# In a first layer's last image, the norm's weights and the residual sum move from GpSimd to VectorE, and projections use two PSUM pairs

## The chip, the cores and the metric

The kernel is one program on one core of a Trainium2 chip. The core has four compute engines that run side by side, each through its own instructions in order: TensorE (PE in the rows) multiplies matrices, VectorE (DVE) and ScalarE (ACT) work elementwise and reduce, GpSimd (POOL) works elementwise on SBUF. SyncE (SP) issues the transfers (DMA). An instruction can wait for a semaphore to reach a count, and raise one when it is done. The metric is the device time of one execution in microseconds (us), the median of several.

## What is computed

Two layers on x, 16 images of 128x128 positions with 128 channels, all f32. The change lies in the first, a linear attention with a norm behind it and the input added:

```python
qkv = einsum('bxyc,cf->bxyf', groupnorm(x), w_qkv)      # 4 heads of 32
q = softmax(q, over the head) * scale;  k = softmax(k, over the positions)
context = einsum('bhdn,bhen->bhde', k, v)
out = einsum('bhde,bhdn->bhen', context, q) @ w_out + b_out
x1 = x + (out - mean) / sqrt(var + eps) * g_ln + b_ln    # mean, var over channels
```

The second layer takes x1, normed in groups, through 7x7 convolutions with gates, a scan of 8 steps and a last product. The sums for its norm come out of the first layer.

## The kernel before

The first layer (`layer0`) cuts an image into 16 chunks of 1024 positions (8 tiles of 128), 256 chunks in all. It is a pipeline over three images: while image i+2 is loaded and turned (`ga`), image i+1 gets its keys, queries and context (`gb`), and image i its output (`gc`). Each engine has its own program of 16 steps `n` an image. In step gc of the last image nothing of ga is left, and nothing of gb after its second step, so only this remains:

- TensorE: the gram of chunk gc-3 (`gram_of`, L468: x1 times itself, summed over the image in psG), behind a wait for x1 of that chunk (`s_x1`); then the projection of chunk gc-1 (`project`, L527: queries times the folded matrix M, into psO, which the rows call psProj, one pair of PSUM banks), behind a wait for `s_y`, that the chunk before has been read out of psO.
- ScalarE: the square of the projection (L615).
- VectorE: row sums of the squares of chunk gc-2 (L650), then, behind GpSimd's `rstd`, y = psO times rstd (`scale_rows`, L656), into the single buffer y, behind `s_x1` of the chunk before.
- GpSimd: rstd from the row sums in two operations (L801, L804, 128x8), then y times the norm's weights (L812), then the input chunk xc plus y (L817), which raises `s_x1`. The bias of the norm is accounted for elsewhere.
- SP: loads of xc, one chunk of the input for each step, four buffers; and, behind `s_x1`, the stores of x1 in four or seven transfers.

Two pairs of banks, psR[0] and psR[1], serve turns, keys and queries while there are images behind; in the last image they are idle from the third step on. The order in every engine is that of the code; nothing is scheduled elsewhere. After the last chunk a block of another kind starts (`corner_block`), behind the last stores.

Of the kernel before, what the change touches and what calls it, by code (L numbers as in the profile page):

```python
# [25 lines left out]
ALU = mybir.AluOpType  # L26
ACT = mybir.ActivationFunctionType
AX = mybir.AxisListType

P = 128  # L30
IMGS, HT, WD, C = 16, 128, 128, 128
# [10 lines left out]
TPC = 8  # L42
CT = TPC * P
NCH = N // CT
# [207 lines left out]
def layer0(nc, x, w_qkv, w_out0, b_out0, g_ln, head_d, x1_d, x1s_d, x1e_d, ident, group, sums2):  # L252

    CHUNKS = IMGS * NCH
# [3 lines left out]
    with ExitStack() as ctx:  # L258
# [4 lines left out]
        qT = [sb(f"qT{n}", [P, CT]) for n in range(NCH)]  # L263
        xa = [sb(f"xa{k}", [P, TPC, C]) for k in range(2)]
        xb = [sb(f"xb{k}", [P, TPC, C]) for k in range(2)]
        xc = [sb(f"xc{k}", [P, TPC, W1]) for k in range(4)]
# [3 lines left out]
        sqo = sb("sqo", [P, TPC, C])  # L270
        y = sb("y", [P, TPC, C])
# [7 lines left out]
        grow = sb("grow", [P, C])  # L279
# [13 lines left out]
        M = sb("M", [P, C])  # L293
# [16 lines left out]
        psR = [ps(f"psR{k}", [P, CT]) for k in range(2)]  # L310
        psO = ps("psProj", [P, CT])
# [8 lines left out]
        s_xc = [sem(f"b_xc{k}") for k in range(4)]  # L320
# [38 lines left out]
        s_y = sem("b_y")  # L359
        s_yg = sem("b_y_gained")  # L360
        s_x1 = sem("b_x1")
# [6 lines left out]
        def live(img, chunk):  # L368
            return not isinstance(img, int) or 0 <= chunk < CHUNKS

        def image_live(img):
            return not isinstance(img, int) or 0 <= img < IMGS

        def upto(count):
            return max(0, min(count, CHUNKS)) if isinstance(count, int) else count

# [68 lines left out]
        def _(pe):  # L445
# [74 lines left out]
            def project(img, n, gc):  # L520
                m = (n - 1) % NCH
                if m == 0:
                    pe.wait_ge(s_mready, img + 1)
                pe.wait_ge(qt_taken, gc)
                pe.wait_ge(s_y, upto(gc - 1))
                for t in range(TPC):
                    mm = nc.tensor.matmul(psO[:, t * C:(t + 1) * C], qT[m][:, t * P:(t + 1) * P], M[:],  # L527
                                          start=True, stop=True)
                mm.then_inc(o_ready, 1)

# [54 lines left out]
        @block.scalar  # L585
        def _(act):
            def image(img, steps):
                for n in range(steps):
                    ga, gb, gc = indices(img, n)
                    if live(img, gb - 2):  # L590
                        act.wait_ge(qt_ready, gb - 1)
                        act.wait_ge(o_ready, upto(gc - 1))
                        nc.scalar.copy(qT[(n - 2) % NCH][:], psR[n % 2][:]).then_inc(qt_taken, 1)
                    if live(img, gb - 1):
                        act.wait_ge(e_ready, gb)
                        act.wait_ge(ctx_done, upto(gb - 1))
                        nc.scalar.copy(ek[:].rearrange("p t c -> p (t c)"), psR[(n + 1) % 2][:]).then_inc(ek_ready, 1)
                        act.wait_ge(q_subbed, gb)
                        v = q[(n - 1) % 2]
                        nc.scalar.activation(v[:], v[:], ACT.Exp).then_inc(s_qexp, 1)  # L600
                    if live(img, gb):
                        act.wait_ge(s_nmax, gb + 1)
                        act.wait_ge(e_ready, upto(gb))
                        nc.scalar.activation(ekT[:], psR[n % 2][:], ACT.Exp, bias=nmax[:, n + 1:n + 2],  # L604
                                             accum_out=ksum_c[:, n:n + 1]).then_inc(k_exped, 1)
                        nc.scalar.activation(corr[:, n:n + 1], nmax[:, n:n + 1], ACT.Exp, bias=nmax[:, n + 1:n + 2],
                                             scale=-1.0).then_inc(s_corr, 1)
                    if n == 0 and image_live(img):
                        act.wait_ge(s_m, img * 7 + 3)
                        nc.scalar.activation(ctxg[:], psC[:, 128:256], ACT.Identity, bias=norm_old[:, 1:2],  # L610
                                             scale=norm_old[:, 0:1]).then_inc(s_m, 1)
                    if live(img, gc - 1):
                        act.wait_ge(o_ready, gc)
                        act.wait_ge(s_vsum, upto(gc - 1))
                        nc.scalar.activation(sqo[:].rearrange("p t c -> p (t c)"), psO[:], ACT.Square  # L615
                                             ).then_inc(s_sqo, 1)
                    if live(img, ga):
                        act.wait_ge(t_taken, ga)
                        act.wait_ge(t_ready, ga + 1)
                        act.wait_ge(q_ready, upto(gb + 1))  # L620
                        if image_live(img + 1):
                            act.wait_ge(s_red, img + 2)
                        src = psR[n % 2][:]
                        nc.scalar.activation(junk[:], src, ACT.Square, accum_out=part_sums[:, 1, n:n + 1])
                        nc.scalar.activation(xT[n][:], src, ACT.Identity, accum_out=part_sums[:, 0, n:n + 1]
                                             ).then_inc(t_taken, 1)

            all_images(act, image)

        @block.vector  # L630
        def _(dve):
            t = Tally(dve, s_chain)
# [19 lines left out]
            def scale_rows(n, gc):  # L652
                dve.wait_ge(s_rstd, gc - 1)
                dve.wait_ge(s_x1, upto(gc - 2))
                rs = rstd[:, n % 2, :].unsqueeze(2).to_broadcast([P, TPC, C])
                nc.vector.tensor_tensor(y[:], psO[:].rearrange("p (t c) -> p t c", c=C), rs, ALU.mult  # L656
                                        ).then_inc(s_y, 1)

            def reduce_sums(gb):
                dve.wait_ge(t_taken, gb + NCH)  # L660
# [91 lines left out]
            def image(img, steps):  # L752
                for n in range(steps):
                    ga, gb, gc = indices(img, n)
                    if live(img, gc - 2):
                        row_sums(img, n, gc)
                    if n == 0 and image_live(img):
                        nc.vector.tensor_copy(norm_old[:], norm[:])
                    if n == 0 and image_live(img + 1):
                        reduce_sums(gb)  # L760
                    if n == 1 and image_live(img):
                        dve.wait_ge(s_m, img * 7 + 5)
                        nc.vector.tensor_tensor(ctxT[:], psC[:, 256:384], head[:], ALU.mult).then_inc(s_m, 1)
                    if live(img, gc - 2):
                        scale_rows(n, gc)
                    if n == 1 and image_live(img):
                        dve.wait_ge(s_m, img * 7 + 7)
                        dve.wait_ge(o_ready, img * NCH)
                        nc.vector.tensor_tensor(M[:], psC[:, 384:512], brow[:], ALU.add).then_inc(s_mready, 1)
                    if n == 2 and image_live(img - 1):  # L770
                        take_gram(img, gc)
                    if n == 0 and image_live(img + 1):
                        norm_weights(img, gb)
                    if n == 0 and live(img, gb - 1):
                        add_up(n, gb)
                        mean_context(img, gb)
                    if n == 0 and image_live(img + 1):
                        split_bias(img)
                    if live(img, gb):
                        max_k(n, gb)  # L780
                    if live(img, gb - 1):
                        sum_q(n, gb)
                        if n:
                            add_up(n, gb)
                    if live(img, gb):
                        centre_q(n, gb)
# [4 lines left out]
        def _(pool):  # L791
# [4 lines left out]
            def image(img, steps):  # L796
                for n in range(steps):
# [8 lines left out]
                    if n == 0 and image_live(img + 1):  # L806
                        pool.wait_ge(s_st, (img + 1) * 5 + 4)
                        nc.gpsimd.tensor_tensor(norm[:, 0:1], var[:], half[:, 0:1], ALU.pow).then_inc(s_pow, 1)
                    if live(img, gc - 2):
                        m, owner = (n - 2) % NCH, img if n >= 2 else img - 1  # L810
                        pool.wait_ge(s_y, gc - 1)
                        nc.gpsimd.tensor_tensor(y[:], y[:], grow[:].unsqueeze(1).to_broadcast([P, TPC, C]), ALU.mult  # L812
                                                ).then_inc(s_yg, 1)
                        pool.wait_ge(s_yg, gc - 1)
                        pool.wait_ge(s_xc[m % 4], owner * (4 * NCH) + m // 4 * 16 + 16)
                        v = xc[m % 4][:, :, 0:C]
                        nc.gpsimd.tensor_tensor(v, v, y[:], ALU.add).then_inc(s_x1, 1)  # L817
# [735 lines left out]
```

## Time and profile before

| | us |
|---|---|
| median of 3 runs | 6883.95 |
| the three runs | 6856.88 to 6893.54 |
| the profiled execution, its time | 6909.09 |
| its span, first to last instruction | 6907.3 |
| last image's stretch, first projection to last x1 | 3522.28 to 3655.95 |

All rows are of the profiled execution, times counted from its span's start. A chunk number below is that of the whole run: the last image has chunks 240 to 255. PEclk is the granted clock of TensorE as a share of 2.4 GHz.

### The profile page before, as it was taken

What the parts mean: (1) busy time and instruction counts of PE and PEld (TensorE: products, weight loads), DVE (VectorE), ACT (ScalarE), POOL (GpSimd) and SP (SyncE); (2) the same over time, 40 slices, a digit from 0 to 9 for tenths busy, and PEclk for the clock granted to TensorE, in tenths of its full rate; (3) what the DMA queues carried; (4) which work ended last, traced back from release to release, by engine and by line L of the source; (5) the groups of instructions that cost most, each with busy time, mean ns of one, the idle gap of its engine ahead of it and who ended that gap; (6) DMA issues with size and microseconds to landing.
All of it is one profiled execution on the core that took longest, in us unless ns stands there. A gap on an engine that the chain in (4) does not pass through costs nothing. (4 is left out here: it accounts for less than half of the span.)

```text
span 6907.3 us, 144255 instructions
## 1 busy us (share of the span) xinstructions
PE 5912.3 (86%) x51796; PEld 5278.5 (76%) x51796; DVE 4477.4 (65%) x5283; ACT 3641.9 (53%) x4872; POOL 4068.1 (59%) x3608
## 2 busy tenths in 40 slices
PE   6799999999999999999871378888888888888898
PEld 5678888888888888888761277777777777777787
DVE  6367777777777777777744556666666666666652
ACT  5655556555555555555421355555555555555552
POOL 0146666666666666666671676676666666666640
PEclk8899999999999999999985699999999999999996
DMA  5356667666677666676561589999999899999985
GB/s 129 122 166 208 198 207 216 198 205 201 202 211 209 203 202 201 204 216 205 169 176 50 148 218 247 243 255 249 257 244 255 241 255 255 244 249 250 251 231 154
DMA packets 1239334, 1441.35 MB, mean 209 GB/s; under 512 B 142960, under 2 KB 1025396, under 8 KB 1238516
## 3 DMA queue, kind: packets, MB, share of 16 engines
q1 hardware_dynamic: 1238516, 1431.07, 73.4%
q8 instruction: 437, 7.16, 0.4%
q14 instruction: 381, 3.12, 0.1%
HBM read 999.09 MB, written 431.64 MB: 207 GB/s over the span
## 5 line engine op out<-in xcount | busy, mean ns | idle before, releaser
L1283 PE MATMUL psC<-wide,xhl 128*128 128x256 bf16 x6144 | 1042.9, 280 | 198.6 <-DVE xhl L1451 170.4
L1220 POOL TENSOR_TENSOR stage<-stage,nrow 128x1024 f32<-128x1024 f32 x256 | 652.3, 2549 | 597.7 <-DMA stage<-x_by_block_row 583.0
L1280 PE MATMUL psC<-wide,xhl 128*128 128x192 bf16 x6144 | 868.6, 251 | 0.0
L1237 POOL COPY down<-xhl 48x448 f32<-48x448 f32 x512 | 522.5, 1021 | 545.6 <-PE psC L1289 486.4
L812 POOL TENSOR_TENSOR y<-y,grow 128x1024 f32<-128x1024 f32 x256 | 604.0, 2359 | 323.7 <-DVE y L656 323.7
L1283 PEld LDWEIGHTS psC<-wide,xhl 128*128 128x128 bf16 x6144 | 593.6, 115 | 210.0 <-issue 195.1
L1456 DVE SCALAR_TENSOR_TENSOR xhl<-xhl,psC 128x512 f32<-128x512 f32 x512 | 348.9, 682 | 540.4 <-ACT xhl L1372 539.9
L1387 ACT ACTIVATE hT<-psH 128x512 f32<-128x512 f32 x512 | 305.2, 596 | 700.0 <-PE psH L1325 699.7
L823 POOL TENSOR_TENSOR q<-q,qinv 128x1024 f32<-128x1024 f32 x256 | 490.1, 1914 | 309.4 <-DVE qinv L730 309.4
L1372 ACT ACTIVATE xhl<-psC 128x512 f32<-128x512 f32 x512 | 304.8, 599 | 664.0 <-PE psC L1289 662.5
L1289 PE MATMUL psC<-narrow,down 128*128 128x96 bf16 x6144 | 532.5, 211 | 143.0 <-DMA narrow<-toeplitz_narrow 94.9
L1280 PEld LDWEIGHTS psC<-wide,xhl 128*128 128x128 bf16 x6144 | 641.8, 115 | 14.4
L656 DVE TENSOR_TENSOR y<-psProj,rstd 128x1024 f32<-128x1024 f32 x256 | 313.5, 1225 | 516.1 <-POOL rstd L804 516.1
L615 ACT ACTIVATE sqo<-psProj 128x1024 f32<-128x1024 f32 x256 | 263.2, 1028 | 707.7 <-PE psProj L527 707.7
L1338 PE MATMUL psO<-w,hT 128*128 128x128 f32 x4096 | 636.1, 302 | 0.0
L1338 PEld LDWEIGHTS psO<-w,hT 128*128 128x128 f32 x4096 | 533.5, 203 | 127.1 <-issue 127.1
L491 PEld LDWEIGHTS psCtx<-xb,ek 128*128 128x128 f32 x4096 | 497.3, 192 | 140.8 <-issue 74.7
L1289 PEld LDWEIGHTS psC<-narrow,down 128*128 128x128 bf16 x6144 | 449.3, 116 | 166.3 <-issue 115.9
L817 POOL TENSOR_TENSOR xc<-xc,y 128x1024 f32<-128x1024 f32 x256 | 558.8, 2183 | 25.2 <-POOL y L812 9.9
L1440 DVE TENSOR_TENSOR stage<-stage,nrow 128x1024 f32<-128x1024 f32 x256 | 336.0, 1313 | 364.5 <-POOL stage L1220 364.4
L604 ACT ACTIVATE ekT<-psR,nmax 128x1024 f32<-128x1024 f32 x256 | 285.4, 1115 | 541.4 <-DVE nmax L721 541.4
L516 PEld LDWEIGHTS psR<-wqk,xT 128*128 128x128 f32 x4096 | 543.5, 193 | 28.4 <-issue 7.7
(166 smaller groups left out, 14383.7 us busy)
## 6 DMA issues: line engine op xcount, KB each, us to landing
wide<-toeplitz_wide SPq DMA_DIRECT2D x1024, 140.0 KB, 4.3
xa<-in_x SPq DMA_DIRECT2D x256, 512.0 KB, 4.6
xb<-in_x SPq DMA_DIRECT2D x256, 512.0 KB, 3.8
xc<-in_x SPq DMA_DIRECT2D x256, 512.0 KB, 5.7
x_rows<-xc SPq DMA_DIRECT2D x256, 512.0 KB
res<-x_rows SPq DMA_DIRECT2D x256, 512.0 KB, 7.4
out<-res SPq DMA_DIRECT2D x256, 512.0 KB, 6.4
stage<-x_by_block_row SPq DMA_DIRECT2D x240, 512.0 KB, 7.1
```

Of the source, the lines that this page charges most:

```text
L491: mm = nc.tensor.matmul(psC[:, 0:C], ek[:, t, :], xb[k][:, t, :], start=(t == 0), stop=(t == TPC - 1))
L516: mm = nc.tensor.matmul(out[:, t * P:(t + 1) * P], xT[n][:, t * P:(t + 1) * P], wqk[:, 0:C], start=False, stop=(t % 4 == 3))
L812: nc.gpsimd.tensor_tensor(y[:], y[:], grow[:].unsqueeze(1).to_broadcast([P, TPC, C]), ALU.mult).then_inc(s_yg, 1)
L817: nc.gpsimd.tensor_tensor(v, v, y[:], ALU.add).then_inc(s_x1, 1)
L823: nc.gpsimd.tensor_tensor(qv, qv, iv, ALU.mult).then_inc(s_qn, 1)
L1220: nc.gpsimd.tensor_tensor(v, v, nrow[:, 0:1, :].to_broadcast([P, NP_, C]), ALU.mult).then_inc(s_scaled, 1)
L1237: nc.gpsimd.tensor_copy(dst[lo, :, :, 0:last], src[lo, :, 0:NQ, CW:])
L1280: nc.tensor.matmul(dst[:, :, :, 2:], lhs, tab[:, :, 32 + part * 12:44 + part * 12], start=False, stop=False)
L1283: nc.tensor.matmul(dst, lhs, tab[:, :, part * 16:part * 16 + 16], start=(n == 0), stop=False)
L1289: mm = nc.tensor.matmul(dst, down[:, blk % DR, hl, :, ci], narrow[:, blk % NR, :, ci, part * 16:part * 16 + 16], start=False, stop=(n == 2))
L1338: mm = nc.tensor.matmul(psO[:, s * C:(s + 1) * C], hT[:, t % 2, s * P:(s + 1) * P], w[:], start=False, stop=(s == HS - 1))
L1456: nc.vector.scalar_tensor_tensor(tb, tb, 1.0, psC[blk % CR][:, :, 0, :], ALU.add, ALU.mult).then_inc(s_prod, 1)
```

## The change

In the last image only (`closing`), GpSimd's two large operations on a chunk are issued by VectorE (`finish`), in its next step, between the row sums and the scaling of the chunk behind. Odd chunks of that image are projected into psR[0] instead of psO, and a projection waits for the scaling of the chunk two before it, not one.

```diff
+        def closing(chunk):
+            return isinstance(chunk, int) and (IMGS - 1) * NCH <= chunk < CHUNKS
+
+        def projected(chunk):
+            return psR[0] if closing(chunk) and chunk % 2 else psO
...
-                pe.wait_ge(s_y, upto(gc - 1))
+                pe.wait_ge(s_y, gc - 2 if closing(gc - 2) else upto(gc - 1))
+                out = projected(gc - 1)
                 for t in range(TPC):
-                    mm = nc.tensor.matmul(psO[:, t * C:(t + 1) * C], qT[m][:, t * P:(t + 1) * P], M[:],
+                    mm = nc.tensor.matmul(out[:, t * C:(t + 1) * C], qT[m][:, t * P:(t + 1) * P], M[:],
                                           start=True, stop=True)
...
+            def finish(c):
+                k = c % 4
+                dve.wait_ge(s_y, c + 1)
+                nc.vector.tensor_tensor(y[:], y[:], grow[:].unsqueeze(1).to_broadcast([P, TPC, C]), ALU.mult
+                                        ).then_inc(s_yg, 1)
+                dve.wait_ge(s_yg, c + 1)
+                dve.wait_ge(s_xc[k], c // 4 * 16 + 16)
+                v = xc[k][:, :, 0:C]
+                nc.vector.tensor_tensor(v, v, y[:], ALU.add).then_inc(s_x1, 1)
...
+                    if closing(gc - 3):
+                        finish(gc - 3)
                     if live(img, gc - 2):
                         scale_rows(n, gc)
...
-                    if live(img, gc - 2):
+                    if live(img, gc - 2) and not closing(gc - 2):
                         m, owner = (n - 2) % NCH, img if n >= 2 else img - 1
                         pool.wait_ge(s_y, gc - 1)
                         nc.gpsimd.tensor_tensor(y[:], y[:], grow[:].unsqueeze(1).to_broadcast([P, TPC, C]), ALU.mult
```

ScalarE's square and VectorE's scaling read `projected(...)` too.

VectorE's rows of before, from the scaling of chunk 240 to that of 241; the four between are those that take the gram of the image before:

```order
L656 TENSOR_TENSOR y<-psProj,rstd 128x1024 [waits b_x1,b_rstd]
L744 COPY gsum<-psGram 128x1 [waits b_gram]
L745 TENSOR_TENSOR gram<-psGram,ident 128x128
L747 TENSOR_REDUCE gsum<-gram 128x1 [waits b_gram_masked]
L750 COPY sums2<-gsum 128x2 [waits b_gram_masked]
L650 TENSOR_REDUCE vsum<-sqo 128x8 [waits b_sqo]
L656 TENSOR_TENSOR y<-psProj,rstd 128x1024 [waits b_x1,b_rstd]
```

VectorE's rows of the changed program between the same places (L657 is the row sums, L663 the scaling, L669 and L674 are new):

```order
L663 TENSOR_TENSOR y<-psProj,rstd 128x1024 [waits b_x1,b_rstd]
L761 COPY gsum<-psGram 128x1 [waits b_gram]
L762 TENSOR_TENSOR gram<-psGram,ident 128x128
L764 TENSOR_REDUCE gsum<-gram 128x1 [waits b_gram_masked]
L767 COPY sums2<-gsum 128x2 [waits b_gram_masked]
L657 TENSOR_REDUCE vsum<-sqo 128x8 [waits b_sqo]
L669 TENSOR_TENSOR y<-y,grow 128x1024 [waits b_y]
L674 TENSOR_TENSOR xc0<-xc0,y 128x8x128 [waits b_xc0,b_y_gained]
L663 TENSOR_TENSOR y<-psR0,rstd 128x1024 [waits b_x1,b_rstd]
```

Between the row sums of a chunk and its scaling there now stand the multiplication and the addition of the chunk before.

TensorE's rows of before in the middle of the last image, two steps: grams of chunks 241 and 242 (xc1, xc2), projections of 243 and 244 (qT3, qT4):

```order
L468 MATMUL psGram<-xc1 128x129 [waits b_x1]
L468 MATMUL psGram<-xc1 128x129 x7
L527 MATMUL psProj<-M,qT3 128x128 [waits b_y,b_q_taken]
L527 MATMUL psProj<-M,qT3 128x128 x7
L468 MATMUL psGram<-xc2 128x129 [waits b_x1]
L468 MATMUL psGram<-xc2 128x129 x7
L527 MATMUL psProj<-M,qT4 128x128 [waits b_y,b_q_taken]
L527 MATMUL psProj<-M,qT4 128x128 x7
```

The same two steps of the changed program (L474 is the gram, L534 the projection):

```order
L474 MATMUL psGram<-xc1 128x129 [waits b_x1]
L474 MATMUL psGram<-xc1 128x129 x7
L534 MATMUL psR0<-M,qT3 128x128 [waits b_y,b_q_taken]
L534 MATMUL psR0<-M,qT3 128x128 x7
L474 MATMUL psGram<-xc2 128x129 [waits b_x1]
L474 MATMUL psGram<-xc2 128x129 x7
L534 MATMUL psProj<-M,qT4 128x128 [waits b_y,b_q_taken]
L534 MATMUL psProj<-M,qT4 128x128 x7
```

The order is the same, gram ahead of projection in each step; the projection of the odd chunk 243 has another target, psR0.

## Rows read from the trace of the kernel before

**Rows 1.** The page: busy time, share of the span and instructions of each engine

```profile
PE 5912.3 (86%) x51796; PEld 5278.5 (76%) x51796; DVE 4477.4 (65%) x5283; ACT 3641.9 (53%) x4872; POOL 4068.1 (59%) x3608
```

**Rows 2.** Windows: stretch, length, PE, PEld, DVE, ACT, POOL busy, PEclk, DMA, GB/s

```profile
3450.00:3500.00 50.00, 46.30 (x357) 41.47 (x356) 36.85 (x42) 22.61 (x30) 34.31 (x22) 1.00 0.60 173
3550.00:3600.00 50.00, 30.67 (x194) 28.23 (x193) 15.68 (x13) 7.17 (x7) 39.91 (x25) 0.86 0.66 185
```

**Rows 3.** Timeline of one step: start, length, engine, line, names [idle<-releaser]

```profile
3632.11 2.05 PE L468 MATMUL psGram<-xc 128*128 128x129 f32 x16 [2.57 <-POOL xc L817]
3633.98 1.22 DVE L656 TENSOR_TENSOR y<-psProj,rstd 128x1024 f32<-128x1024 f32 x1 [2.12 <-POOL rstd L804]
3635.28 2.35 POOL L812 TENSOR_TENSOR y<-y,grow 128x1024 f32<-128x1024 f32 x1 [1.34 <-DVE y L656]
3635.35 2.02 PE L527 MATMUL psProj<-M,qT 128*128 128x128 f32 x16 [1.18 <-DVE y L656]
3637.41 1.02 ACT L615 ACTIVATE sqo<-psProj 128x1024 f32<-128x1024 f32 x1 [6.80 <-PE psProj L527]
3638.46 1.22 DVE L650 TENSOR_REDUCE vsum<-sqo 128x8 f32<-128x1024 f32 x1 [3.26 <-ACT sqo L615]
3639.84 0.21 POOL L801 TENSOR_TENSOR rstd<-vsum,ceps 128x8 f32<-128x8 f32 x1
3639.94 3.01 PE L468 MATMUL psGram<-xc 128*128 128x129 f32 x16 [2.57 <-POOL xc L817]
3640.13 1.64 POOL L804 TENSOR_TENSOR rstd<-rstd,minus_half 128x8 f32<-128x8 f32 x1
3641.80 1.22 DVE L656 TENSOR_TENSOR y<-psProj,rstd 128x1024 f32<-128x1024 f32 x1 [2.12 <-POOL rstd L804]
```

**Rows 4.** Groups by line, 3538 to 3656 us: count, busy us, mean ns, idle

```profile
L468 PE MATMUL psGram<-xc 128*128 128x129 f32 x227 | 40.4, 349 | 33.1 <-POOL xc L817 33.1
L527 PE MATMUL psProj<-M,qT 128*128 128x128 f32 x224 | 31.1, 296 | 7.6 <-DVE y L656 7.3
```

**Rows 5.** Timeline, TensorE in two pairs of steps of that stretch

```profile
3544.11 2.77 PE L468 MATMUL psGram<-xc 128*128 128x129 f32 x16 [2.56 <-POOL xc L817]
3547.34 2.66 PE L527 MATMUL psProj<-M,qT 128*128 128x128 f32 x16 [0.46 <-DVE y L656]
3623.85 3.64 PE L468 MATMUL psGram<-xc 128*128 128x129 f32 x16 [2.04 <-POOL xc L817]
3627.52 2.02 PE L527 MATMUL psProj<-M,qT 128*128 128x128 f32 x16
```

**Rows 6.** Timeline, the first chunks of the last image

```profile
3526.76 2.51 PE L468 MATMUL psGram<-xc 128*128 128x129 f32 x16 [2.43 <-POOL xc L817]
3528.68 1.22 DVE L656 TENSOR_TENSOR y<-psProj,rstd 128x1024 f32<-128x1024 f32 x1 [2.04 <-POOL rstd L804]
3530.05 3.75 PE L527 MATMUL psProj<-M,qT 128*128 128x128 f32 x16 [0.78 <-DVE y L656]
3538.16 1.23 DVE L656 TENSOR_TENSOR y<-psProj,rstd 128x1024 f32<-128x1024 f32 x1 [2.04 <-POOL rstd L804]
```

**Rows 7.** Timeline, the end of the layer and the next block

```profile
3645.53 2.17 POOL L817 TENSOR_TENSOR xc<-xc,y 128x1024 f32<-128x1024 f32 x1
3650.06 1.23 DVE L656 TENSOR_TENSOR y<-psProj,rstd 128x1024 f32<-128x1024 f32 x1 [2.04 <-POOL rstd L804]
3653.78 2.17 POOL L817 TENSOR_TENSOR xc<-xc,y 128x1024 f32<-128x1024 f32 x1
3656.01 3.81 PE L468 MATMUL psGram<-xc 128*128 128x129 f32 x16 [6.21 <-POOL xc L817]
```

**Rows 8.** VectorE: two operations in a row, and one line's min/median/max ns

```profile
3501.38 1.21 DVE L735 TENSOR_REDUCE qmax<-psR 128x32 f32<-128x1024 f32 x1
3502.62 1.22 DVE L740 TENSOR_TENSOR q<-psR,qmax 128x1024 f32<-128x1024 f32 x1
L1440 DVE TENSOR_TENSOR stage<-stage,nrow x256: 1209/1226/3344, 3812.9 to 6590.4; 128x1024 f32<-128x1024 f32 x128
```

More of the change, by code:

```diff
@@ L614, in image @@
                         act.wait_ge(s_vsum, upto(gc - 1))
-                        nc.scalar.activation(sqo[:].rearrange("p t c -> p (t c)"), psO[:], ACT.Square
+                        nc.scalar.activation(sqo[:].rearrange("p t c -> p (t c)"), projected(gc - 1)[:], ACT.Square
                                              ).then_inc(s_sqo, 1)
@@ L655, in scale_rows @@
                 rs = rstd[:, n % 2, :].unsqueeze(2).to_broadcast([P, TPC, C])
-                nc.vector.tensor_tensor(y[:], psO[:].rearrange("p (t c) -> p t c", c=C), rs, ALU.mult
+                nc.vector.tensor_tensor(y[:], projected(gc - 2)[:].rearrange("p (t c) -> p t c", c=C), rs, ALU.mult
                                         ).then_inc(s_y, 1)
+            def finish(c):
[7 more added lines that the diff above has]
+                nc.vector.tensor_tensor(v, v, y[:], ALU.add).then_inc(s_x1, 1)
             def reduce_sums(gb):
```

## The prediction

> **What bounds the kernel now.** I began with the page. TensorE is busy 86% of the span, VectorE 65%, GpSimd 59% [rows 1], but that is an average over two layers, and the change touches only the stretch in which the first layer works on its last image. So I read the windows next. While two images overlap, a stretch of 50 us has TensorE busy 46.3 us at granted clock 1.00. In the last image, where no newer image is left to load or turn, it is busy 30.7 us at clock 0.86, VectorE 15.7 us, ScalarE 7.2 us, and GpSimd 39.9 us, the most of any engine [rows 2]. Nobody is full; a loop of dependences sets the pace.
>
> The timeline of one step shows the loop [rows 3]. I write G(c) for the gram of chunk c (L468), P(c) for its projection (L527), S for the square (L615), R for the row sums (L650), Y for the scaling (L656), M for the multiplication by the norm's weights (L812), A for the addition of x (L817). Y starts at 3633.98. M starts 1.30 later and takes 2.35; A follows and takes 2.17 [rows 3, 7]; the two rstd operations take 0.21 and 1.64, and the next Y starts at 3641.80. So a step is 7.82 us, and four fifths of it is GpSimd: M, A, rstd, rstd. P, S and R of the next chunk run beside M and A: P starts 1.37 after Y and R ends at 3639.68, only 0.16 before the rstd that needs it. The clock shows too. In some steps G and P take 2.77 or 3.64 instead of 2.05 [rows 5], R comes late, and the step is longer: from Y(241) at 3538.16 to Y(255) at 3650.06 are 14 steps, 7.99 us each [rows 6, 7]. The number to beat is 7.99.
>
> **What is removed.** For 16 chunks GpSimd loses M and A, 4.52 us a step. It keeps the rstd pair. With the old loop gone, those are behind R and ready about 2.1 us after it (Y's idle time in [rows 3]).
>
> **What is added.** VectorE gets M and A, 32 operations of 128x1024 f32 with both inputs in SBUF. The trace of before has no such operation in this stretch. The nearest row is L1440, the same shape, type and memory: minimum 1.209, median 1.226 us, and a maximum of 3.344 [rows 8]; GpSimd was at its large operations there, and here it has only 1.85 us of small ones a step. I take 1.22 each. The handover between two dependent VectorE operations is 3502.62 less 3501.38 + 1.21, that is 0.03 [rows 8]. VectorE's own work in a step is then four operations of 1.22, 5.0 us with handovers: alone that would be much faster than 7.99.
>
> **What is moved.** P(c) no longer waits for Y(c-1), since odd chunks have a second pair of banks. But A moves too: from GpSimd, right behind Y(c), into VectorE's next step, behind R(c+1). And TensorE's order is unchanged: G(c-2) stands ahead of P(c). In the step that brings P(c), G(c-2) now waits for A(c-2), which VectorE runs after R(c-1). That closes a new loop, with nothing beside it:
>
> A(c-2) ends, G(c-2), P(c), S(c), R(c), M(c-1), A(c-1) ends.
>
> Before, G(c-2) ran in the shadow of GpSimd's rstd and P(c) in that of M. Now both matmul groups, the square, the row sums and both new operations stand in one line. Step by step at full clock:
>
> - A's end to G: 0.14, as from Y's end (3635.20) to P (3635.35) [rows 3]
> - G 2.05; P 2.02 and 0.04 to S [rows 3]
> - S start to R start 1.05 [rows 3]
> - R 1.22, M 1.22, A 1.22, with two handovers of 0.03 [rows 3, 8]
>
> The sum is 9.02 us. Y(c-1) and the rstd pair are off this line: R, then M and A (2.5 us) cover rstd's 2.1, and Y runs beside G. With that cover gone rstd's 2.1 would still lie beside G and P, 4.1. SP issues the same transfers in the same order, a longer step gives it more time, and in this stretch no idle time ahead of G or P is put down to a transfer [rows 4]; I count it at nothing.
>
> **The clock.** TensorE now idles from the end of P to the next G: 0.04 + 1.05 + 3.7 + 0.14 = 4.9 us in every step. Before, the pause ahead of G is 2.57 in the step shown [rows 3], and G and P already took 40.4 and 31.1 us [rows 4] where 15 at 2.05 and 14 at 2.02 make 59.0: 12.5 us of delay. The one G that came after 6.21 us of idling ran its 16 passes in 3.81, half rate, 1.2 GHz [rows 7]. When the clock fell, the pair G and P took 3.64 + 2.02 = 5.66 [rows 5], so it came back to 2.4 GHz during the pair; others fell to 2.77 + 2.66. So I take a fall in every step, and an extra of 1.4 us for it (the first pair's is 5.66 - 4.07 = 1.59; 1.4 is what the 2.77 + 2.66 kind gives, 5.43 - 4.07 = 1.36). The step is 10.4 us. The bounds are no fall, 9.02, and no recovery at all, where G costs 3.81 and P 3.75 [rows 6, 7]: 12.5.
>
> On this the Trainium skill speaks against the change: "TensorE: Matmul & The Clock Gate", section "Why this matters for your kernels", asks for no pauses between bursts of matmuls, or the clock falls back to half. The row after 6.21 us agrees. By that rule the step is the 10.4, without it 9.0.
>
> **The sum.** G(239) starts at 3526.76 as now and ends at 3529.27; P(241) goes to the other pair at once and, at the low clock of its row, takes 3.75 [rows 6]. Then 0.04, 1.05, 1.22 + 1.22 + 1.22 and handovers: A(240) ends at 3537.8. A(254) ends 14 steps later, at 3537.8 + 14 x 10.4 = 3683.4. A last Y, M, A of 3.74 ends the image at 3687.1. Before, A(255) ended at 3653.78 + 2.17 = 3655.95 [rows 7]. The image grows by **31 us**. What follows (stores of the last chunk, the corner block) starts from A(255) in both. The final G and GpSimd's freeing of VectorE give at most 2 us, which I leave out. The profiled execution took 6909.09 and becomes 6940; it was 25 us above the median of the three runs shown, 6883.95, from which I forecast **6915 us**, +0.45%.
>
> **The rivals.**
> - *The clock stays up* (chance 0.12). The step is 9.02: 3537.8 + 126.3 + 3.7 = 3667.8, +12 us, 6896. For it: the pair in [rows 3] ran at full rate. Against: a pause twice as long now.
> - *The clock never recovers* (0.07). Step 12.5: 3716.5, +61 us, 6945. For it: P(241) and the G after 6.21 us ran wholly at half rate. Against: each regular pair shown [rows 5] ended faster than half rate.
> - *Faster: VectorE alone sets the pace* (0.05). If TensorE took P(c) without waiting for G(c-2), the four operations would: 5.0 us a step, 3537.8 + 70 + 3.7 = 3611.5, -44 us, 6840. It decides from the step of (3655.95 - 3.74 - 3537.8)/14 = 8.17 us: any loop shorter than that is a gain. Against: TensorE's rows of the changed program have G first, with its wait for x1, in each step. The Trainium skill ("TensorE: Matmul & The Clock Gate", "What happens when you issue a matmul") says that only weight loads are pulled ahead, matmuls stay in program order; no row here shows a P ahead of its G.
> - My forecast, the loop with a falling clock: 0.76.
>
> **How the numbers follow.** A measurement of this kernel tells about 0.5%, 34 us, from no change; the three runs shown spread over 37 us. The forecast of +31 lies just inside. With an extra for the clock between 0.9 and 2.2 us a step it spans +24 to +43, and the runs' own spread comes on top, so of its 0.76 I give 0.45 to within 0.5%, 0.31 to slower. The full clock adds 0.11 to the same and 0.01 to slower, no recovery 0.07 to slower, VectorE's pace 0.05 to faster: faster 0.05, same 0.56, slower 0.39. The range runs from 6878 (the full clock's 6896 less half a spread) to 6946 (the half clock's).
>
> **What would show it.** In the profile after: L474's gram starts 0.1 to 0.2 behind VectorE's addition, L534's projection right behind the gram, with no wait for y; VectorE idle some 5 us a step, before L657, released by the square; L669 and L674 at 1.22; steps of 10.4 (Y to Y), with GpSimd down to 1.85 us of work in each. It is wrong if the projection starts ahead of the gram, if the new operations take near 0.7 or above 2 us, or if the gram of a step is at 2.05 throughout.

## The result and the profile after

The change made the kernel slower: 6926.28 us median of 12 runs (6888.57 to 6935.20) against 6875.10 of 12 runs before (6856.88 to 6893.54); ratio 1.0066, 95% interval 1.0049 to 1.0083. That is 34 to 57 us. The profiled execution took 6934.65 us against 6909.09, and has a span of 6932.9.

The page, which answers to [rows 1]: VectorE has gained 54 us of work and GpSimd lost 63, TensorE and ScalarE stay within 4. The windows view puts 35 and 47 of these ahead of the next block's start; most of the rest lies in the second layer, whose busy times also differ between two executions of the changed kernel (VectorE 1974 and 1942 us, GpSimd 1926 and 1947).

```profile
PE 5915.8 (85%) x51796; PEld 5283.8 (76%) x51796; DVE 4531.5 (65%) x5315; ACT 3640.8 (53%) x4872; POOL 4005.2 (58%) x3576
```

The windows view of the last image (columns as in [rows 2]): GpSimd has gone from 39.9 to 18.6 us in 50, VectorE from 15.7 to 23.6, TensorE from 30.7 to 27.4. No engine is now as busy as GpSimd was.

```profile
3550.00:3600.00 50.00, 27.38 (x160) 26.43 (x160) 23.61 (x20) 4.38 (x5) 18.63 (x10) 0.83 0.57 161
```

The timeline of one step, from an addition to the next (answers to [rows 3]):

```profile
3551.99 1.23 DVE L674 TENSOR_TENSOR xc<-xc,y 128x1024 f32<-128x1024 f32 x1
3552.09 2.62 POOL L823 TENSOR_TENSOR rstd<-rstd,minus_half 128x8 f32<-128x8 f32 x1
3553.27 3.33 PE L474 MATMUL psGram<-xc 128*128 128x129 f32 x16 [4.76 <-DVE xc L674]
3554.74 1.22 DVE L663 TENSOR_TENSOR y<-psR,rstd 128x1024 f32<-128x1024 f32 x1 [1.53 <-POOL rstd L823]
3556.39 2.35 PE L534 MATMUL psProj<-M,qT 128*128 128x128 f32 x16
3558.78 1.02 ACT L622 ACTIVATE sqo<-psProj 128x1024 f32<-128x1024 f32 x1 [9.21 <-PE psProj L534]
3559.84 1.22 DVE L657 TENSOR_REDUCE vsum<-sqo 128x8 f32<-128x1024 f32 x1 [3.87 <-ACT sqo L622]
3560.97 1.22 DVE L669 TENSOR_TENSOR y<-y,grow 128x1024 f32<-128x1024 f32 x1
3561.14 1.11 POOL L820 TENSOR_TENSOR rstd<-vsum,ceps 128x8 f32<-128x8 f32 x1 [6.43 <-DVE vsum L657]
3562.22 1.22 DVE L674 TENSOR_TENSOR xc<-xc,y 128x1024 f32<-128x1024 f32 x1
```

Read it down. The addition ends at 3553.22 and the gram starts at 3553.27, after 4.76 us of idling; the projection follows it without a wait; the square starts with the projection's end, the row sums 1.06 later, then the multiplication and the next addition, which starts 10.23 after the first. Nothing on this line has slack. Y, at 3554.74, lies beside the gram. The two new operations cost what L1440 said; the view of their lines (min/median/max ns):

```profile
L674 DVE TENSOR_TENSOR xc<-xc,y x16: 1224/1224/1226, 3531.0 to 3680.1; 128x1024 f32<-128x1024 f32 x16
L669 DVE TENSOR_TENSOR y<-y,grow x16: 1214/1215/1225, 3529.8 to 3678.8; 128x1024 f32<-128x1024 f32 x16
```

The first chunk and the end of the layer (answer to [rows 6, 7]; L963 is the next block's first operation on VectorE):

```profile
3525.62 1.95 PE L534 MATMUL psR<-M,qT 128*128 128x128 f32 x16
3525.66 1.23 DVE L663 TENSOR_TENSOR y<-psProj,rstd 128x1024 f32<-128x1024 f32 x1 [2.03 <-POOL rstd L823]
3532.33 3.81 PE L474 MATMUL psGram<-xc 128*128 128x129 f32 x16 [4.76 <-DVE xc L674]
...
3674.82 1.22 DVE L674 TENSOR_TENSOR xc<-xc,y 128x1024 f32<-128x1024 f32 x1
3677.57 1.22 DVE L663 TENSOR_TENSOR y<-psR,rstd 128x1024 f32<-128x1024 f32 x1 [1.53 <-POOL rstd L823]
3680.09 1.22 DVE L674 TENSOR_TENSOR xc<-xc,y 128x1024 f32<-128x1024 f32 x1
3689.44 0.23 DVE L963 TENSOR_SCALAR cross<-sums,bln_col 128x16 f32<-128x16 f32 x1 [5.10 <-PEq L258]
```

From Y(240), 3525.66, to the end of A(255), 3681.31, are 155.65 us; before, 3655.95 - 3528.68 = 127.27. The stretch grew by 28.4 us. Its 14 steps from Y(241), 3533.80, to Y(255), 3677.57, take 10.27 us on average in place of 7.99: the first 10.70, behind the gram of 3.81, and the others 10.24. From Y(240) to the next block it is 163.8 against 135.4 (that operation was at 3664.10 before).

### The profile page after: what moved, and what is told of

It reads as the page before. It is cut to its first block and busy times, and to the rows that moved or that the text cites. A ratio compares the mean times of both kernels' runs of the same rounds, so it can differ in the third digit from the quotient of the medians.

```text
span 6932.9 us, 144255 instructions
## 1 busy us (share of the span) xinstructions
PE 5915.8 (85%) x51796; PEld 5283.8 (76%) x51796; DVE 4531.5 (65%) x5315; ACT 3640.8 (53%) x4872; POOL 4005.2 (58%) x3576
## 5 line engine op out<-in xcount | busy, mean ns | idle before, releaser
L831 POOL TENSOR_TENSOR y<-y,grow 128x1024 f32<-128x1024 f32 x240 | 565.3, 2355 | 302.2 <-DVE y L663 302.2
L663 DVE TENSOR_TENSOR y<-psProj,rstd 128x1024 f32<-128x1024 f32 x248 | 303.6, 1224 | 493.9 <-POOL rstd L823 493.9
L474 PE MATMUL psGram<-xc 128*128 128x129 f32 x4096 | 529.7, 284 | 75.8 <-DVE xc L674 73.3
L474 PEld LDWEIGHTS psGram<-xc 128*128 128x128 f32 x4096 | 504.1, 200 | 79.1 <-DVE xc L674 76.5
```

Source lines behind the costliest of these rows:

```text
L474: mm = nc.tensor.matmul(psG[:, 0:W1], v[:, t, 0:C], v[:, t, :], start=(m == 0 and t == 0), stop=(m == NCH - 1 and t == TPC - 1))
```

## The experiments

Each kernel was profiled once and timed against the kernel before on the same chip. "Step" is Y(241) to Y(255), divided by 14; "stretch" is Y(240) to the next block's first operation on VectorE, both from the kernel's own trace. The ratio carries the spread of the whole kernel, the stretch does not.

| kernel | step us | stretch us | ratio to before, 95% |
|---|---|---|---|
| before | 7.99 | 135.4 | |
| f3: before again | 7.93 | 133.4 | 0.9991 (0.9969 to 1.0012) |
| changed | 10.27 | 163.8 | 1.0066 (1.0049 to 1.0083) |
| f4: changed again | 10.24 | 163.3 | 1.0049 (1.0025 to 1.0074) |
| e1: projection ahead of gram | 7.01 | 131.8 | 0.9998 (0.9981 to 1.0016) |
| e2: M and A ahead of row sums | 7.31 | 133.5 | 0.9986 (0.9967 to 1.0004) |
| e3: 12 filler matmuls | 10.24 | 165.0 | 1.0069 (1.0045 to 1.0094) |
| f2: 18 filler matmuls | 8.60 | 140.4 | 1.0030 (1.0013 to 1.0046) |
| e4: move without the second pair | 10.20 | 164.3 | 1.0056 (1.0036 to 1.0077) |
| f1: second pair without the move | 8.26 | 138.1 | 1.0016 (0.9998 to 1.0033) |
| g1: e1, ScalarE stores rows | 6.48 | 117.7 | 0.9981 (0.9964 to 0.9998) |
| g2: e2, ScalarE stores rows | 7.02 | 117.2 | 0.9976 (0.9958 to 0.9993) |

**e1, the projection ahead of the gram.** On top of the change, in TensorE's step:

```diff
+                    if closing(gc - 2) and live(img, gc - 1):
+                        project(img, n, gc)
                     if live(img, gc - 3):
                         gram_of(img, n, gc)
...
-                    if live(img, gc - 1):
+                    if live(img, gc - 1) and not closing(gc - 2):
                         project(img, n, gc)
```

> The changed kernel, but in the last image TensorE issues the projection of chunk c ahead of the gram of chunk c-2. If the loop A, G, P, S, R, M, A sets the step of 10.24 us (my theory), taking P out from behind G and A breaks it, and VectorE with GpSimd's rstd sets the pace: in the changed kernel R to Y start is 5.14 us, with Y 1.25 behind it, so a step near 6.4 to 6.6 us, 14 steps some 52 us shorter than changed and 20 us shorter than before. If instead the new VectorE work or its contention with GpSimd is the cause (rival), the order changes nothing or only a few us: step 9 to 10.2.

Timeline of a step of its first half, and three rows of its second:

```profile
3562.46 2.02 PE L534 MATMUL psR<-M,qT 128*128 128x128 f32 x16 [0.79 <-DVE y L665]
3563.52 1.11 POOL L822 TENSOR_TENSOR rstd<-vsum,ceps 128x8 f32<-128x8 f32 x1 [2.46 <-DVE vsum L659]
3564.60 1.22 DVE L676 TENSOR_TENSOR xc<-xc,y 128x1024 f32<-128x1024 f32 x1
3564.71 2.62 POOL L825 TENSOR_TENSOR rstd<-rstd,minus_half 128x8 f32<-128x8 f32 x1
3565.88 2.05 PE L474 MATMUL psGram<-xc 128*128 128x129 f32 x16 [1.40 <-DVE xc L676]
3567.36 1.22 DVE L665 TENSOR_TENSOR y<-psProj,rstd 128x1024 f32<-128x1024 f32 x1 [1.53 <-POOL rstd L825]
...
3602.89 1.11 POOL L822 TENSOR_TENSOR rstd<-vsum,ceps 128x8 f32<-128x8 f32 x1 [5.23 <-DVE vsum L659]
3604.08 1.64 POOL L825 TENSOR_TENSOR rstd<-rstd,minus_half 128x8 f32<-128x8 f32 x1
3607.80 1.23 DVE L676 TENSOR_TENSOR xc<-xc,y 128x1024 f32<-128x1024 f32 x1 [3.85 <-DMA xc<-in_x]
```

The projection runs beside R, M and A, and the steps there are 6.27 us, Y to Y (3561.09, 3567.36, 3573.62), though VectorE does the same work as in the changed kernel: the loop was the cause. What sets the 6.27 is the line Y, R, the rstd pair at 1.11 + 2.62, and the next Y. The expectation held for these steps and missed the total. In the second half additions wait for x. The waits view of 3536 to 3660 (total, times, longest) and the window 3590 to 3640:

```profile
DVE xc L676 <- DMA xc<-in_x: 23.9, 7, 4.8
```

```profile
3590.00:3640.00 50.00, 27.17 (x160) 25.92 (x160) 27.21 (x23) 4.71 (x5) 15.14 (x11) 0.79 0.67 190
```

SP issues both the stores of a chunk and the next load of x, and waits ahead of that load until the stores it has just issued, which free the buffer, have landed. The waits view of its queue, 3540 to 3640:

```profile
SPq L422 <- DMA x_first_column<-xc: 21.1, 12, 3.6
```

In the same 100 us it waited for an addition once, for 0.3: SP's own round, 8.56 us from load to load, is now the slower one. After A(255) ends (3642.61) it still issues the stores of three chunks, almost without a break, until 3658.99, and 18 us pass until the next block, 8 before. The stretch ends 2 to 4 us below the kernel before, not 20.

**e2, M and A ahead of the row sums.** On top of the change, VectorE's step:

```diff
+                    if closing(gc - 3):
+                        finish(gc - 3)
                     if live(img, gc - 2):
                         row_sums(img, n, gc)
...
-                    if closing(gc - 3):
-                        finish(gc - 3)
                     if live(img, gc - 2):
                         scale_rows(n, gc)
```

> The changed kernel, but VectorE runs M and A of chunk c-1 ahead of the row sums of chunk c in its step, TensorE as changed. By the loop theory A no longer waits for S and R of a projection that itself waits for A, and the step is M + A + R + the rstd pair + Y, 1.25 + 1.25 + 1.22 + 2.1 + 1.25 = 7.1 us: some 44 us below the changed kernel and 12 below before. The rstd pair should fall back from 1.11 + 2.62 to 0.2 + 1.64, if it was large two-input operations of VectorE beside them that slowed them. If contention or VectorE's load set the pace, the step stays above 9 and the pair stays slow.

```profile
3567.55 1.21 DVE L657 TENSOR_REDUCE vsum<-sqo 128x8 f32<-128x1024 f32 x1
3568.85 0.20 POOL L820 TENSOR_TENSOR rstd<-vsum,ceps 128x8 f32<-128x8 f32 x1 [4.99 <-DVE vsum L657]
3569.13 1.64 POOL L823 TENSOR_TENSOR rstd<-rstd,minus_half 128x8 f32<-128x8 f32 x1
3570.79 1.22 DVE L663 TENSOR_TENSOR y<-psProj,rstd 128x1024 f32<-128x1024 f32 x1 [2.03 <-POOL rstd L823]
3573.31 1.23 DVE L674 TENSOR_TENSOR xc<-xc,y 128x1024 f32<-128x1024 f32 x1
```

In this timeline the rstd pair is back at 0.20 and 1.64, and the step is the line M, A, R, rstd, Y: 6.90 where x is there (3563.89 to 3570.79), 7.31 over 14. That is another way to open the same loop, with TensorE's order left as it was. The 30 us below the changed kernel are less than the 44 expected: 10 of the difference are stores, which again take 18 us behind the last addition in place of 8, and some 3 are steps in which the addition waited for x (6.1 us in 4 waits).

**e3 and f2, filler for the pause.** Behind each projection of the last image (f2 has 18 for 12); these products are extra work that nothing reads:

```diff
+                if closing(gc - 2):
+                    for t in range(12):
+                        nc.tensor.matmul(psC[:, 384:512], qT[m][:, 0:P], M[:], start=True, stop=True)
```

> The changed kernel with 12 more matmuls of 128x128 f32 behind each projection of the last image, into an unused part of psCtx; nothing reads them. They fill some 3 us of the 4.8 us that TensorE idles ahead of each gram. If the falling clock costs 1.4 us a step, gram and projection go back to 2.05 and 2.02 and the step to 8.8 us, about 20 us below the changed kernel, still 10 above before. If the clock is no part of it (rival), the step stays 10.2 or grows by what the filler delays.

> As e3_filler, with 18 matmuls in place of 12, some 4.3 us, so that TensorE is idle about 0.5 us ahead of a gram. If a falling clock is worth 1.4 us a step, it now stays at 2.4 GHz, gram and projection take 2.05 and 2.02 and the step is 8.8 us, 20 us less than the changed kernel in the stretch. If the step of 10.24 has another cause, it stays or grows.

Windows and timeline of e3, 12 matmuls (L539 is the filler):

```profile
3540.00:3650.00 110.00, 87.14 (x595) 85.05 (x594) 52.80 (x44) 10.68 (x11) 40.99 (x22) 0.83 0.56 157
```

```profile
3564.62 3.70 PE L474 MATMUL psGram<-xc 128*128 128x129 f32 x16 [2.08 <-DVE xc L677]
3568.12 1.98 PE L534 MATMUL psR<-M,qT 128*128 128x128 f32 x16
3569.94 2.84 PE L539 MATMUL psCtx<-M,qT 128*128 128x128 f32 x24
3574.86 1.56 PE L474 MATMUL psGram<-xc 128*128 128x129 f32 x6 [2.08 <-DVE xc L677]
```

And of f2, 18:

```profile
3540.00:3650.00 110.00, 100.40 (x870) 97.92 (x870) 61.91 (x52) 13.22 (x13) 48.45 (x26) 1.00 0.65 185
```

```profile
3570.43 2.05 PE L474 MATMUL psGram<-xc 128*128 128x129 f32 x16 [0.74 <-DVE xc L677]
3572.32 1.95 PE L534 MATMUL psProj<-M,qT 128*128 128x128 f32 x16
3574.10 4.18 PE L539 MATMUL psCtx<-M,qT 128*128 128x128 f32 x36
3579.03 2.05 PE L474 MATMUL psGram<-xc 128*128 128x129 f32 x16 [0.74 <-DVE xc L677]
```

With 12 the pause ahead of the gram is 2.08 us, and nothing is gained: clock 0.83, gram 3.70. That was a miss; the shorter pause still let the clock fall in every step. With 18 the pause is 0.74, the clock 1.00, gram and projection 2.05 and 1.95, and the step 8.60. So the loop at 2.4 GHz costs 8.60, and the falling clock 10.24 - 8.60 = 1.64 a step, some 23 us over 14. All of it lies in the pair: from the gram's start to the projection's end are 5.47 us in the changed kernel, 5.48 in e3 and 3.84 in f2. Even at full clock this loop is slower than the 7.99 of the kernel before.

**e4, the move without the second pair.** `projected` returns psO, and the projection waits for `upto(gc - 1)` as before.

> The changed kernel without the second PSUM pair: every projection goes to psO and waits for the scaling of the chunk just before. By the loop theory the scaling of c-1 ends about 2.8 us after A, while the gram ahead of the projection takes 3.3 us, so the wait is hidden: step 10.2, within 5 us of the changed kernel. If the second pair was worth something (rival), the step grows towards 11 and the time by 10 us.

```profile
3566.35 1.23 DVE L674 TENSOR_TENSOR xc<-xc,y 128x1024 f32<-128x1024 f32 x1
3567.63 3.66 PE L474 MATMUL psGram<-xc 128*128 128x129 f32 x16 [4.76 <-DVE xc L674]
3569.10 1.22 DVE L663 TENSOR_TENSOR y<-psProj,rstd 128x1024 f32<-128x1024 f32 x1 [1.53 <-POOL rstd L823]
3571.13 1.95 PE L534 MATMUL psProj<-M,qT 128*128 128x128 f32 x16
```

As the loop has it: Y starts at 3569.10 and ends 0.8 us ahead of the projection, which follows the gram. The step is 10.20, so the move alone is the whole loss, and the second pair carries nothing here.

**f1, the second pair without the move.** `finish` is not called and GpSimd keeps M and A.

> The kernel before with the second PSUM pair alone; GpSimd keeps M and A. The projection starts behind the gram instead of behind Y, so the row sums are never late for rstd, and a step is the 7.82 us of GpSimd and Y in each step instead of 7.99 on average: 2 to 3 us less in the stretch, no difference in the time. A rival, that the pair itself or the missing pause costs something, would have steps above 8.

```profile
3561.40 3.81 PE L474 MATMUL psGram<-xc 128*128 128x129 f32 x16 [3.96 <-POOL xc L834]
3565.00 2.64 PE L534 MATMUL psProj<-M,qT 128*128 128x128 f32 x16
3568.74 1.22 DVE L657 TENSOR_REDUCE vsum<-sqo 128x8 f32<-128x1024 f32 x1 [4.25 <-ACT sqo L622]
3570.04 0.20 POOL L818 TENSOR_TENSOR rstd<-vsum,ceps 128x8 f32<-128x8 f32 x1 [0.88 <-DVE vsum L657]
```

A miss: 8.26 a step, not 7.82. The projection now follows the gram closely, so that TensorE idles in one piece. In every second step the clock falls, and both are slow (3.81 and 2.64 here); the row sums then end late, here at 3569.96, and GpSimd has waited 0.88 for them. The second pair spares the projection its wait, but the row sums come no earlier when gram and projection run at the lower clock. In the whole time f1 is not to be told from the kernel before.

**f3 and f4, both kernels again.**

> The kernel before, unchanged, as a kernel of its own. Ratio 1.000 within 0.2%. The stretch from Y(240) to the next block's first operation 135.4 us as in the first profile, within 2; what differs between executions lies in the second layer.

> The changed kernel, unchanged, on the same chip as the kernel before. The stretch from Y(240) to the next block 163.8 us within 2, so 28 us above before; if the first layer's end is all that differs the ratio is 1.004, and 1.0066 as first measured held some 15 us of the second layer's own spread. If the ratio is again 1.0065 or more with this stretch, something behind it is slower too.

The stretches repeat within some 2 us. The ratio of the changed kernel is 1.0049, an interval of 17 to 51 us, which holds the 28 to 30 of the stretch; the first interval, 34 to 57, does not. What lies behind the stretch, from that operation to the end of the span, took 3243.2 and 3232.8 us in the two profiles of before, 3243.5 and 3207.5 in those of after: 36 us between two executions of one kernel. The mean granted clock behind the stretch was 0.91 in the two long ones of 3243 us, 0.92 in the one of 3232.8 and 0.93 in the one of 3207.5.

**g1 and g2, a version below both.** On top of e1 and of e2, ScalarE issues one of a chunk's transfers, SP leaves it out:

```diff
+                    if closing(gc - 2):
+                        m, k = (n - 2) % NCH, (n - 2) % 4
+                        act.wait_ge(s_x1, gc - 1)
+                        nc.scalar.dma_start(x1_d[IMGS - 1].rearrange("(n h) (q t) c -> n (h q) t c",
+                                                                     h=ROWS_CH, t=TPC)[m],
+                                            xc[k][:, :, 0:C]).then_inc(s_store[k], 16)
```

> e1_project_first, and in the last image ScalarE issues the store of x1 by rows (one of the 4 or 7 transfers of a chunk) in place of SP. In e1 the steps began at 6.27 us and grew to 8 when additions began to wait for loads of x (23.9 us in 7 waits), with the transfers' share of their engines at 0.67; after the last addition 18 us of stores were left. If SP's issuing is what is behind, SP saves 0.7 us of some 7.3 in each step, the steps stay nearer 6.3 and the next block starts some 8 to 10 us earlier than in e1. If it is the landing of stores and loads in turn, little changes, 0 to 3 us.

> The same with e2_finish_first, whose own step is 6.9 to 7.3 us. If SP's issuing is behind, the stretch from Y(240) to the next block falls from 133.5 to about 126 us, 9 below before; otherwise it stays at 131 to 134. In the time 9 us is 0.13%, hardly to be told from nothing.

The waits view of g1, 3536 to 3665, against 23.9 us in e1:

```profile
DVE xc L683 <- DMA xc<-in_x: 10.0, 4, 3.8
```

And that of its SP queue, 3540 to 3640:

```profile
SPq L422 <- DMA x_first_column<-xc: 26.7, 11, 4.5
```

The stretch falls by 14 to 16 us against e1 and e2 and stands 16 to 18 below the kernel before; both ratios lie below 1 with their intervals, g1's only just. This is more than the 7 to 10 expected. In g1 the last addition ends 8.5 us earlier (105.2 behind Y(240), 113.7 in e1), and the stores behind it take 12.5 us in place of 18.2, which I had not counted. SP's round is down from 8.56 to 7.85, the 0.7 of the expectation. The transfers' engines were not what bound in e1: in the window 3590 to 3640 their share rises from 0.67 to 0.77 in g1. But SP's round is more than issuing: it still waits for its stores to land, 26.7 us of 100. That one transfer fewer on SP shortens the round is shown; what an earlier landing of that transfer adds is not told apart.

## Why the prediction held

**The loop.** Shown. The line A, G, P, S, R, M, A is in the trace as written, and two edits that open it at different places, with the same VectorE work, bring the step from 10.2 to 6.3 and 6.9 where x is there. e4 shows that the move alone closes it.

**Its price at full clock.** I summed 9.02; f2 has 8.60. A's end to G is 0.05, not 0.14; S, R, M and A follow one another a little faster, since M starts 1.13 after R and not 1.25; and P starts 1.89 behind G and takes 1.95.

**The clock.** I took a fall in every step at 1.4 us; it is a fall in every step at 1.64. The step came out at 10.24 to 10.27 against 10.4 because two errors, 0.42 too much for the loop and 0.24 too little for the clock, mostly cancel. The mechanism was as forecast; that the step came so close is in part luck. That the clock comes back during the pair held (G 3.33, P 2.35). Where I argued from the pause of 4.9 us I was right for this kernel, but e3 shows that a pause of 2.1 does as much in this loop.

**The start and the end.** P(241) ran at 1.95, not 3.75, and the gram ahead of it started earlier; A(240) ended 6.6 us after Y(240), not 9.1. The last Y, M, A took the forecast 3.74, but Y(255) starts 1.53 behind the end of A(254) (3676.04), since it waits for the rstd pair. I had it start at once.

**The sum.** +31 for the image; the trace has +28.4: 2.5 less at the start, 1.8 less in the 14 steps, 1.5 more at the end. The step that was off is the last one, from the stretch to the whole time: 6915 against a median of 6926, inside the range. The first ratio asks for 34 to 57 us, the stretch gives 28 to 30. The repeat is consistent with the stretch alone, yet f2 too has a ratio (9 to 32 us) above its stretch (5 to 7), and e3's (31 to 65) barely reaches down to its 30 to 32; the other ratios agree with their stretches. So I can't rule out that some 10 us more come from outside the stretch. No profile shows it: the part behind took 3201.7 to 3243.5 us in the ten profiles other than the two of before, which had 3232.8 and 3243.2. It stays open. The sign came out as the less likely of the two I weighed, slower by over 0.5%, within the forecast mechanism.

**The rstd pair.** I counted 1.85 us; it takes 1.11 + 2.62. So M and A did not cover it, and Y starts 1.53 behind A in every step. That is beside the gram and off the line, so it cost nothing in the steps, 1.5 us once at the end, and it sets e1's step. Two of my signs were off by it: GpSimd has 3.73 us of work a step, not 1.85, and VectorE's idle time, given as some 5 us ahead of L657, is 3.87 there and 1.53 ahead of Y.

**The rival on the faster side.** Its price was wrong: VectorE alone was to give 5.0 us a step and -44. With P freed, e1 has 6.27, from the slower rstd, and then SP's round of issuing and waiting takes over: -2 to -4. I had counted the transfers at nothing because nobody waited for them; that told of a step of 8, not of 6.

## What to carry to other kernels

Moving work from the busiest engine to an idle one pays only if it doesn't close a longer loop than the one it opens: write down what the moved instruction stands behind on its new engine, and who waits for it, all the way round, before adding up the engines' loads. Here four VectorE operations of 1.2 us made a step of 10.2, and swapping two entries in one engine's order took a third of that away. And before reckoning a large gain, ask how much slack the queue that issues the transfers has at the new pace.

## What the runs showed of the hardware

GpSimd's operations of 128x8 took 0.20 and 1.64 us, but 1.11 and 2.62 beside VectorE's multiplications and additions (M and A) with both inputs in SBUF. In e1's later rows one of them is alone: L822, begun 0.16 behind M, takes 1.11, while L825 at 3604.08, with no such operation beside it, takes 1.64. In e2, where they run beside nothing, both are short. The Trainium skill, "SBUF — State Buffer", section "Who interferes with whom", says that a VectorE instruction with two SBUF inputs and a GpSimd instruction that reads SBUF hold each other up, the second until the first is done. The trace agrees: L820 in the step above starts at 3561.14, inside M (3560.97 to 3562.19), and ends at 3562.25. I had not weighed it.

TensorE's clock: a pause of 2.08 us ahead of each gram (e3) let it fall in every step as one of 4.76 did in the changed kernel, both at a mean of 0.83; with 0.74 (f2) it stayed at 1.00. The length of the one pause does not settle it: in f1 the gram at 3553.60 came after 2.49 us of idling and still took 2.05, while those after 3.96 to 5.38 took 3.81.
